# Three of the six chunks of each expert tile's down product as three fp32r products of high and low halves, the weights' low halves made by GpSimd

## What is computed

```python
def _expert(h, g, u, d):
    return jnp.einsum('...i,hi->...h', jax.nn.silu(h @ g.T) * (h @ u.T), d)
probs = jax.nn.softmax(x @ wr.T + rb, axis=-1)
scores, idx = jax.lax.top_k(probs, 2)
scores = scores / scores.sum(axis=-1, keepdims=True)
w = jnp.sum(scores[..., None] * jax.nn.one_hot(idx, 7, dtype=x.dtype), axis=-2)
for e in range(7):
    out = out + w[..., e:e + 1] * _expert(x, rg[e], ru[e], rd[e])
```

## Time and profile before

| | us |
|---|---|
| median of 3 runs | 1199.94 (1197.11 to 1203.04) |
| the profiled execution | 1197.35 |
| its span in the profile | 1195.5 |
| TensorE busy | 1064.4 (89%) |
| VectorE / ScalarE / GpSimd busy | 629.3 / 617.3 / 392.1 |
| routed stage, from the first tile's down product to the last but one | 42 of them, from 495.9 to 819.1 |

### The profile page before, as it was taken

The page is one execution under the profiler, slowest core; times in us unless marked ns, Lnnn a source line. Parts: engine busy times, 40 slices in busy tenths (PEclk is TensorE's granted clock), DMA queues, the critical chain, the costliest instruction groups (busy, mean ns, idle before and its releaser), DMA issues.

```text
span 1195.5 us, 28362 instructions
## 1 busy us (share of the span) xinstructions
PE 1064.4 (89%) x10404; PEld 901.1 (75%) x10405; DVE 629.3 (53%) x1174; ACT 617.3 (52%) x1043; POOL 392.1 (33%) x271
## 2 busy tenths in 40 slices
PE   6988799888988887899999999995678899789998
PEld 5877677766766665788888888884467777689998
DVE  3337577643332324566666666662257766734443
ACT  3446566643533432455555555553255557556554
POOL 1155344424534443022221122222455455611110
PEclk9999899998998988899999999998789989889999
DMA  6550000053101112101110101102311000000000
GB/s 230 199 225 3 4 2 3 3 221 109 29 20 23 26 21 70 46 31 35 35 35 31 35 31 35 35 31 67 111 27 39 22 0 2 2 1 21 20 10 32
DMA packets 31010, 57.45 MB, mean 48 GB/s; under 512 B 13084, under 2 KB 22506, under 8 KB 29780
## 3 DMA queue, kind: packets, MB, share of 16 engines
q1 hardware_dynamic: 16376, 44.06, 11.1%
q0 software_dynamic: 13328, 10.66, 3.3%
q10 hardware_dynamic: 1228, 1.60, 0.4%
HBM read 41.51 MB, written 14.67 MB: 47 GB/s over the span
## 4 chain that ended last, share of the span: by engine, by line
PE 58%; DVE 11%; issue 9%; POOL 9%; ACT 9%; DMA 3%; SPq 0%; DVEq 0%; ACTq 0%; POOLq 0%
PE ps L1197 20%; PE ps L1202 11%; PE ps L1204 10%; PE ps L1203 10%; POOL routed_in L462 7%; DVE Sb L854 6%; PE ps L1576 2%; DVE mx L849 2%; ACT RTs L624 2%; PE ps L1308 1%; DMA x_in<-in_xT_dram 1%; ACT vts L604 1%; ACT RTs L622 1%; PE ps L1319 1%; ACT prs L610 1%
## 5 line engine op out<-in xcount | busy, mean ns | idle before, releaser
L486 POOL DMA_INDIRECT routed_out<-yt,tile_to x43 | 65.4, 1521 | 289.5 <-DVE yt L1132 285.3
L1110 DVE TENSOR_TENSOR tile_w<-arena,tile_w 128x1408 fp32r<-128x1408 f32 x86 | 139.3, 1621 | 35.6 <-ACT tile_w L784 35.6
L1197 PE MATMUL ps<-arena,shared 128*128 x516 | 130.9, 395 | 1.0 <-ACT shared L780 1.0
L1202 PE MATMUL ps<-tile_w,xTs 128*128 128x352 f32 x344 | 120.1, 349 | 2.4 <-DVE xTs L1115 2.4
L784 ACT ACTIVATE tile_w<-arena 128x1408 fp32r x86 | 118.2, 1375 | 6.5 <-issue 6.5
L949 DVE TENSOR_TENSOR Hd<-Sg,ps 128x296 f32<-128x296 f32 x96 | 44.3, 462 | 140.1 <-ACT Sg L725 135.4
L773 ACT ACTIVATE shared<-ps 128x352 f32<-128x352 f32 x86 | 39.8, 463 | 145.8 <-PE ps L1204 141.4
L1204 PE MATMUL ps<-tile_w,xTs 128*128 128x352 f32 x344 | 112.0, 326 | 0.0
L1197 PEld LDWEIGHTS ps<-arena,shared 128*128 128x128 f32 x516 | 90.9, 189 | 28.0 <-issue 15.6
L1203 PE MATMUL ps<-tile_w,xTs 128*128 128x352 f32 x344 | 111.9, 325 | 0.0
L389 POOL TENSOR_TENSOR xn<-cen,rsd 128x592 f32<-128x592 f32 x32 | 46.7, 1460 | 191.1 <-ACT rsd L572 191.0
(11 more groups left out here) (195 smaller groups left out, 2673.1 us busy)
## 6 DMA issues: line engine op xcount, KB each, us to landing
arena<-in_ew_dram SPq DMA_DIRECT2D x7, 2176.0 KB, 13.4
x_in<-in_xT_dram SPq DMA_DIRECT2D x7, 888.0 KB, 5.7
xt<-routed_in SPq DMA_DIRECT2D x43, 129.0 KB, 2.0
yg<-routed_out SPq DMA_DIRECT2D x8, 512.0 KB
out_dram<-h SPq DMA_DIRECT2D x8, 296.0 KB, 2.7
routed_in<-zero_x SPq DMA_DIRECT2D x13, 129.0 KB, 10.3
gu_i<-in_gu_dram SPq DMA_DIRECT2D x1, 1536.0 KB, 10.2
shared<-in_gu_dram SPq DMA_DIRECT2D x1, 1408.0 KB, 7.4
```

Source lines behind the costliest of these rows:

```text
L486: pool.indirect_dma_start(ys, bass.IndirectOffsetOnAxis(tile_to[b][:, 0:1], 0), yt[b][:], None).then_inc(s_yt, 16)
L1110: dve.tensor_tensor(tile_w[half][1], gate_up_of(w, half), tile_w[half][0].bitcast(F32), ALU.subtract).then_inc(s.wl, 1)
L1197: return pe.matmul(out_, lhsT, rhs, start=start, stop=stop)
L1202: pe.matmul(out_, w[1], x[0], start=start, stop=False)
```

## The change

Chunks 0 to 2 of the down product become `mm3` products; chunks 3 to 5 stay `mm`, and are now first. For that

- ScalarE makes `dn_hi`, the high half of the down weights' first three chunks (128 x 768), once per tile at the head of its step, after the down product that used it before (`E.y_mm`). It copies the transposes in three pieces instead of two: `HT_hi` (128 x 384, fp32r), then two pieces of `HTs`.
- VectorE makes `HT_lo` (128 x 384, from PSUM and `HT_hi`) between `lower_weights` and `gate(t, 1)`.
- GpSimd makes `dn_lo` in two instructions (128 x 512 and 128 x 256, reading `arena` and `dn_hi`) at the head of `store(t)`, ahead of the wait for `yt`; it also loads the register with the tile's weight offset.
- TensorE waits for `E.htl` and `E.dl` between the three `mm` and the nine fp32r matmuls.

The core of the diff:

```diff
+SPLIT = 3
...
+                def lower_down(t):
+                    w = weights_of(pool, t)
+                    pool.wait_ge(E.dh, t + 1)
+                    dn_w = down_of(w)
+                    pool.tensor_tensor(dn_lo01, dn_w[:, 0:2], dn_hi[:, 0:2].bitcast(F32), ALU.subtract)
+                    pool.tensor_tensor(dn_lo[2], dn_w[:, 2], dn_hi[:, 2].bitcast(F32), ALU.subtract).then_inc(E.dl, 1)
+
                 def store(t, b):
+                    lower_down(t)
                     pool.wait_ge(E.y, FREE + t + 1)
                     pool.sem_inc(s_turn, 1)
...
                 def hidden_t(t):
 
                     act.wait_ge(s.ht_mm, t + 1)
-                    act.activation(HTs[:, 0:5], ps[:, 4:6, :].rearrange("p b (j m) -> p (b j) m", m=P)[:, 0:5],
-                                   ACT.Copy)
-                    act.activation(HTs[0:I0 - 5 * P, 5], ps[0:I0 - 5 * P, 5, P:2 * P], ACT.Copy).then_inc(s.ht, 1)
+                    in_bank = lambda bk, n: ps[:, bk, 0:n * P].rearrange("p (j m) -> p j m", m=P)
+                    act.activation(HT_hi, in_bank(4, SPLIT), ACT.Copy).then_inc(s.ht, 1)
+                    act.activation(HTs[:, 0:5 - SPLIT], in_bank(5, 5 - SPLIT), ACT.Copy)
+                    act.activation(HTs[0:I0 - 5 * P, 5 - SPLIT], ps[0:I0 - 5 * P, 5, 2 * P:3 * P], ACT.Copy).then_inc(s.ht, 1)
+
+                def upper_down(t):
+
+                    w = weights_of(act, t)
+                    act.wait_ge(s.y_mm, t)
+                    act.activation(dn_hi, down_of(w), ACT.Copy).then_inc(s.dh, 1)
...
                 def step(t, b, last):
+                    upper_down(t - 1)
...
+                def lower_hidden(t):
+                    dve.wait_ge(s.ht, FREE + 2 * t + 1)
+                    dve.tensor_tensor(HT_lo, ps[:, 4, 0:SPLIT * P].rearrange("p (j m) -> p j m", m=P), HT_hi.bitcast(F32),
+                                      ALU.subtract).then_inc(s.htl, 1)
...
                     gate(t, b, 0)
                     if not last:
                         lower_weights(t + 1, w, 0)
+                    lower_hidden(t - 1)
                     gate(t, b, 1)
...
                 def tile_out(t, w):
-                    pe.wait_ge(s.ht, FREE + t + 1)
+                    pe.wait_ge(s.ht, FREE + 2 * t + 2)
                     pe.wait_ge(s.y, FREE + t)
-                    for j, r in enumerate(hidden_chunks(I0)):
-                        ins = mm(ps[:, 7, 0:D], HTs[0:r, j], arena[0:r, bass.ds(w + DK * 2 * I0 + j * D, D)],
-                                 j == 0, j == 5)
+                    for j, r in list(enumerate(hidden_chunks(I0)))[SPLIT:]:
+                        mm(ps[:, 7, 0:D], HTs[0:r, j - SPLIT], arena[0:r, bass.ds(w + DK * 2 * I0 + j * D, D)],
+                           j == SPLIT, False)
+                    pe.wait_ge(s.htl, FREE + t + 1)
+                    pe.wait_ge(s.dl, t + 1)
+                    for j in range(SPLIT):
+                        ins = mm3(ps[:, 7, 0:D], (HT_hi[:, j], HT_lo[:, j]), (dn_hi[:, j], dn_lo[j]), False, j == SPLIT - 1)
                     ins.then_inc(s.y_mm, 1)
```

More of the change, by code:

```diff
@@ L176, in vit_kernel @@
         Hdt = [shared[:, (1 + b) * I0:(2 + b) * I0] for b in range(2)]
-        HTs = shared[:, 3 * I0:3 * I0 + 6 * P].rearrange("p (j m) -> p j m", j=6)
-        assert 3 * I0 + 6 * P + 4 * D <= EW
+        HTs = shared[:, 3 * I0 + SPLIT * P:3 * I0 + 6 * P].rearrange("p (j m) -> p j m", m=P)
+        HT_hi = nc.alloc_sbuf_tensor_at("HT_hi", [P, SPLIT, P], F32R, offset=shared_at + 4 * 3 * I0)[:]
+        HT_lo = nc.alloc_sbuf_tensor_at("HT_lo", [P, SPLIT, P], F32R, offset=norm_at + 4 * 8 * DK * IH)[:]
+        assert prs_at - norm_at - 4 * 8 * DK * IH >= 4 * SPLIT * P
+        tail_at = shared_at + 4 * (3 * I0 + 6 * P)
+        assert 3 * I0 + 6 * P + D + 4 * D <= EW
         xt = [sb(f"xt{b}", [P, XW]) for b in range(2)]
         yt = [sb(f"yt{b}", [P, D]) for b in range(2)]
+        sg_at = -(-nc.sbuf_base // 32) * 32
         Sg = [sb(f"Sg{b}", [P, N]) for b in range(2)]
         Hd = [sb(f"Hd{b}", [P, N]) for b in range(LAG + 1)]
+        hidden_free = nc.sbuf_base
+        assert hidden_free - sg_at >= 5 * 4 * D and shared_at + 4 * EW - tail_at >= 4 * D
+        dn_hi = nc.alloc_sbuf_tensor_at("dn_hi", [P, SPLIT, D], F32R, offset=sg_at)[:]
+        dn_lo01 = nc.alloc_sbuf_tensor_at("dn_lo01", [P, 2, D], F32R, offset=sg_at + 4 * SPLIT * D)[:]
+        dn_lo2 = nc.alloc_sbuf_tensor_at("dn_lo2", [P, D], F32R, offset=tail_at)[:]
+        dn_lo = [dn_lo01[:, 0], dn_lo01[:, 1], dn_lo2]
         r_w = sb("r_w", [P, DK, EXPERTS])
@@ L228, in vit_kernel @@
         F = [counted(ffn_sems + routing_sems, "f0_"), counted(ffn_sems, "f1_")]
-        E = counted("xt_mm gu_mm ht_mm y_mm wh wl xh xt sg hd ht y stored", "e_")
+        E = counted("xt_mm gu_mm ht_mm y_mm wh wl dh dl xh xt sg hd ht htl y stored", "e_")
         C = counted("mm0 mm1 sum h", "c_")
@@ L241, in gate_up_of, with down_of @@
             return arena[:, bass.ds(w, 2 * DK * I0)].rearrange("p (q i) -> p q i", i=I0)[:, :, half * IH:(half + 1) * IH]
+        def down_of(w):
+            return arena[:, bass.ds(w + DK * 2 * I0, SPLIT * D)].rearrange("p (j d) -> p j d", d=D)
         def norms_idle(eng):
@@ L489, in store @@
                     pool.sem_inc(E.stored, 1)
+                norms_idle(pool)
                 with pool.Fori(0, TILES // 2) as i:
@@ L813, in routed @@
                 over_tiles(act, step)
+                upper_down(TILES - 1)
                 hidden_t(TILES - 1)
@@ L1104, in routed @@
                 s = E
-                for buf_free in (s.xt, s.hd, s.y):
+                for buf_free in (s.xt, s.hd, s.y, s.htl):
                     dve.sem_inc(buf_free, FREE)
+                def lower_hidden(t):
+                    dve.wait_ge(s.ht, FREE + 2 * t + 1)
+                    dve.tensor_tensor(HT_lo, ps[:, 4, 0:SPLIT * P].rearrange("p (j m) -> p j m", m=P), HT_hi.bitcast(F32),
+                                      ALU.subtract).then_inc(s.htl, 1)
                 def lower_weights(t, w, half):
@@ L1158, in routed @@
                 over_tiles(dve, step)
+                lower_hidden(TILES - 1)
                 tile_out(TILES - 1, 0)
@@ L1573, in hidden_t @@
                     pe.wait_ge(s.hd, FREE + 2 * t + 2)
-                    pe.wait_ge(s.ht, FREE + t)
+                    pe.wait_ge(s.ht, FREE + 2 * t)
+                    pe.wait_ge(s.htl, FREE + t)
                     for j, r in enumerate(hidden_chunks(I0)):
-                        ins = pe.transpose(ps[0:r, 4 + j // 4, (j % 4) * P:(j % 4 + 1) * P],
+                        ins = pe.transpose(ps[0:r, 4 + j // SPLIT, (j % SPLIT) * P:(j % SPLIT + 1) * P],
                                            Hdt[b][:, j * P:j * P + r], ident)
```

## The result

| | before | changed |
|---|---|---|
| median, us | 1201.49 (4 runs) | 1256.89 (4 runs, 1253.08 to 1258.6) |
| ratio, 95% interval | | 1.0462 (1.0433 to 1.0492) |
| span of the profiled execution | 1195.5 | 1256.2 |
| mean distance of two stores' starts, tiles 0 to 40 | 7.82 | 9.10 |

The change costs 4.6%. The direction was forecast, the size was not: 36 us were forecast, 55 came, and 1256.89 lies above the range (1209 to 1252). Between the two profiled executions lie 60.7 us. Of these, 52.3 lie between the first store and the last but one, where 32.8 were forecast, 4.5 at the end of the stage, 2.3 ahead of the first store and 1.6 behind the last one.

What follows compares the result with a forecast made beforehand. TensorE bounds the kernel before; after the change a ring through GpSimd's store and subtractions does. 41 steps x 0.80 = 32.8 us, plus 3.7 at the end, less 0.4 for the first tile, is 36.1 us: 1236 us, range 1209 to 1252.

Steps and rivals of the forecast that it cites:

- a ring: Routed stage: store, landing, GpSimd's subtractions, nine matmuls, `yt`, next store follow one another, none hidden; 8.62 us a step.
- The ring's length: Time from one store's start to the next in the routed stage: 8.62 instead of 7.81 us, 0.80 more.
- the second of the sum: GpSimd's first subtraction waits for VectorE's L1110, which frees the way at S + 3.9; register load hidden, up to 0.65 us.
- the sign that the register load was too low: Check in the changed kernel's profile: GpSimd's L503 starting later than 0.9 us after the store's landing.
- a rival for a longer ring: Longer register load, VectorE not moving forward or slower subtractions: 0.25 to 0.55 us a step, 1246 to 1258 us; chance 0.12.
- the clock rival: TensorE's idling over 1 us drops its clock to 0.50 in every step: 155 us more, 1355 us; chance 0.05.
- the 1.6 I named: Check: GpSimd's L503 lasts some 1.6 us or more instead of 1.26, beginning before VectorE's L1110 ends.
- the 0.65 of the sum: Wait of GpSimd's subtraction for VectorE's first-half instruction, up to 0.65 us a step, with the register load hidden under it.
- The first rival: GpSimd's subtraction is not held up by VectorE's L1110: 0.15 to 0.45 us a step more, 1209 to 1222 us; chance 0.14.
- TensorE's saving: Down product: three `mm` go, 1.45 us, nine fp32r matmuls come, 1.08 us; TensorE's work falls 0.37 us a tile.
- the faster rival: TensorE stays the bound and its saving of 0.37 us a tile counts: 15.6 us less, 1184 us; chance 0.04.
- The end of the stage: Last result of the routed stage goes around without VectorE's part: 3.1 to 4.3 us more, 3.7 taken.

Runs made afterwards that it cites:

- e1_floor: Changed kernel with GpSimd making the low half of the down weights once, before its loop (stale results); 1193.64 us, 0.9942 of the kernel before.
- e5_before_store: Changed kernel with GpSimd making the next tile's low half ahead of the store; 1195.55 us, 0.9964 of the kernel before.
- e11_load: Changed kernel, three chunks, with TensorE's load of the weight offset moved behind the step's transposes; 1250.28 us, 1.042 of the kernel before.
- e3_no_vector_lock: Changed kernel with VectorE's first-half weight subtraction in the loop on 8 columns instead of 1408; 1247.01 us, 1.0392 of the kernel before.
- e2_no_register: Changed kernel with GpSimd's subtraction at constant offset 0, so it loads no register; 1250.43 us, 1.0415 of the kernel before.
- e6_two_chunks: Changed kernel with two chunks of the six as fp32r products instead of three (SPLIT = 2); 1223.12 us, 1.0168 of the kernel before.
- e4_before_landing: Changed kernel with GpSimd making the next tile's low half after issuing the store, before waiting for its landing; 1209.91 us, 1.0084 of the kernel before.
- e7_no_register_no_vector: Changed kernel with GpSimd at constant offset 0 and VectorE's first-half subtraction on 8 columns; 1217.59 us, 1.0137 of the kernel before.
- e10_two_chunks_load: Changed kernel with two fp32r chunks and TensorE's weight-offset load moved behind the step's transposes; 1204.96 us, 1.0047 of the kernel before.

## Why the prediction was wrong in size

**What bounds, and that a ring forms: right.** TensorE's L1243 was released by L504 before all 42 down products and idled about 1 us; the landing, GpSimd's register load and the subtractions lie in the chain in the order given. VectorE's instruction is not in it, since no semaphore ties it to GpSimd; it shows in the length of L503. e1_floor and e5_before_store show it as the cause.

**The ring's length: 8.62 forecast, 9.10 measured, 0.48 x 41 = 19.5 us, nearly all that the medians lack (55 less 36).** By its steps, for the two turns of the loop:

| from the store's start S | forecast | turn 1 | turn 2 |
|---|---|---|---|
| landing | 3.0 | 2.97 | 2.98 |
| GpSimd ready (start of L503) | 3.25 to 4.1 | 3.94 | 4.18 |
| VectorE's first-half instruction lets go (0.15 before its end) | 3.9 | 4.03 | 4.43 |
| second subtraction ends | 5.85 | 5.99 | 6.39 |
| first fp32r matmul | 5.90 | 6.14 | 6.54 |
| next store | 8.62 | 8.79 | 9.19 |

The step that failed is the second of the sum: VectorE's first-half instruction moves forward with TensorE's step and lets go at S + 3.9, and the register load hides under it up to there. Both halves of it were wrong.

- VectorE's instruction moved forward by 0.13 us in one turn, and back by 0.27 in the other, where TensorE's step starts 0.4 us late, so it let go at S + 4.03 and S + 4.43. It was the later of the two in both turns. The cause I had not seen at all: TensorE's own register load and branch at the head of its step, as I read it hidden behind fp32 passes before and bare after the wait. e11_load takes that gap away. There L1149 lets go at S + 3.95 in both turns, nearly as forecast, and the regular turns are 8.71 and 8.92 us, 0.18 less on average.
- The register load takes 0.73 us, with the loop's branch 0.96, and GpSimd is ready at S + 3.94 and S + 4.18, where 3.9 was the limit. The changed kernel hides this, but it is the floor when VectorE is not in the way: the regular turns of e3_no_vector_lock and e11_load stay at 8.80 and 8.81 us on average, 0.18 over the forecast.

The prediction named a start of L503 later than 0.9 us after the landing as the sign that the register load was too low; it came, with 0.97 and 1.20 us. The wake after GpSimd's signal was 0.15 us instead of 0.05, and from the first fp32r matmul to the next store it took 2.65 us instead of 2.72. I had a rival for a longer ring, 1246 to 1258, by a longer register load or a VectorE that does not move forward, and gave it 0.12. It is what happened, and the result is inside it; its chance was too low.

**Irregular steps.** The mean of the two turns is 8.99; the last 0.1 us a step, some 4 us, comes from single steps. Three take over 10 us and give most of it, 3.6 us. In three others, of 9.45 to 9.66 us, the store took longer to land, as the chain shows for one of them (2.97 us is usual):

```profile
693.32 3.68 DMA routed_out<-yt,tile_to
```

Why these stores land late is open. Two windows of one of the three longest steps show the clock (granted clock is the third number from the end):

```profile
529.00:530.00 1.00, 1.00 (x5) 1.00 (x5) 0.72 (x1) 0.00 (x0) 0.98 (x1) 0.50 0.00 0
531.00:532.00 1.00, 1.00 (x9) 0.93 (x8) 0.00 (x0) 0.40 (x2) 0.00 (x0) 0.76 0.32 131
```

So the clock rival was right in kind in three steps of 42, not in each as it was priced. TensorE's matmuls at half the clock then delay VectorE past GpSimd's first subtraction, and VectorE gets in ahead of the second:

```profile
533.22 1.28 POOL L503 TENSOR_TENSOR dn_lo<-arena,dn_hi 128x512 fp32r<-128x512 f32 x1 [2.63 <-issue]
534.46 2.10 POOL L504 TENSOR_TENSOR dn_lo<-arena,dn_hi 128x256 fp32r<-128x256 f32 x1
...
533.47 2.51 DVE L1149 TENSOR_TENSOR tile_w<-arena,tile_w 128x1408 fp32r<-128x1408 f32 x1 [0.73 <-ACT tile_w L816]
```

**GpSimd's subtraction and VectorE's instruction.** The one waits for the other: right, as the earlier trace rows had it. L503 mostly lasted 1.34 to 1.37 us in one turn and 1.48 to 1.54 in the other, less than the 1.6 I named, because it came late. Nearly taking VectorE's instruction away gave 0.19 us a step alone, not the 0.65 of the sum, because GpSimd, held by its own register load, was ready only 0.1 to 0.25 us earlier than VectorE let go. The first rival (GpSimd comes through beside VectorE) is refuted by e2_no_register, where L503 starts early and takes 2.08 us.

**TensorE's saving: 0.37 forecast, 0.13 measured.** I divided 2.90 us by twelve passes and took 0.242 for each. Six passes fewer took 1.29 us away, 0.215 each, and the first distance behind the fp32 ones is longer than the others (0.22 us instead of 0.12 in e1_floor), which makes 1.16 for nine instead of 1.08. This had no weight in the forecast, since it was hidden, but it made the faster rival, 1184, too good: the best versions reach 1193.6. Per fp32r matmul 0.120 us was right (0.12 measured).

**The end of the stage: 3.7 forecast, 4.5 measured.** The difference is the clock again. Before the last down product TensorE waits 3.75 us for GpSimd, and behind that its granted clock is 0.50 (1.2 GHz). The fp32r matmuls start 0.21 us apart instead of 0.12, which adds some 0.9 us for nine:

```profile
881.08 0.55 PE L1243 MATMUL ps<-dn_hi,HT_lo 128*128 128x256 f32 x1 [3.75 <-POOL dn_lo L504]
881.42 0.41 PE L1244 MATMUL ps<-dn_lo,HT_hi 128*128 128x256 f32 x1
881.64 0.41 PE L1245 MATMUL ps<-dn_hi,HT_hi 128*128 128x256 f32 x1
```

ScalarE and VectorE: their added instructions cost nothing that can be seen, as forecast. The start of the first store, 2.3 us later in the changed kernel's trace, is not explained; in the other runs it lies anywhere between 498.7 and 505.1, so it need not come from the change. The 0.4 us that the first tile was to save would be lost in that.

## What to carry to other kernels

A subtraction on an idle engine is free only where it stands in that engine's order: behind a wait for a DMA's landing it made a ring that no engine's busy time shows. Add up such a ring from the start of one turn to the next, with the register load and the loop's branch of every engine in it, and then look where else in the order the new work can stand; here moving a few lines turned 4.6% lost into 0.5% won. Two waits that end together hide each other: taking away either showed 0.13 to 0.19 us a step, both 0.95. Compare the regular turns too, and not only their mean: there the register load alone was worth 0.02 us.

## What the runs showed of the hardware

- The load of one register from SBUF costs GpSimd 0.73 us between a landing and its next instruction (0.97 to 0.24 with a constant offset). On TensorE it shows behind a wait, at the head of a step: with the loop's branch as a gap of 0.50 us (changed kernel) or 0.73 us (e6_two_chunks) where 0.12 is usual, without the branch not at all in the changed kernel and as 0.39 us in e6_two_chunks. Moved behind the transposes it shows nowhere.
- Two GpSimd instructions in a row can let a waiting instruction of VectorE in between. It got in where it was waiting (L504 2.10 and 2.13 us instead of 0.72), and in other steps of e4_before_landing the second subtraction went first by 0.02 us and VectorE's instruction took 2.20 instead of 1.62 us.
- An indirect DMA on GpSimd takes 2.33 us to issue in e5_before_store, 1.57 in the changed kernel, and 0.98 at 884.68, where VectorE does nothing. The difference is about what VectorE's instruction on two tensors of SBUF still had to run: 1.47 us (602.70 to 604.17) and 0.71 us (611.49 to 612.20).
- TensorE's granted clock fell to 0.50 in three places of the changed kernel's routed stage, with pauses of about 1 us in every step before them, and once more behind the pause of 3.75 us at its end. In e1_floor, without pauses, it stayed at 1.00 from 500 to 800 us, and so it did in e4_before_landing, e6_two_chunks, e7_no_register_no_vector and e10_two_chunks_load, where the pauses are shorter. No run changes the pauses alone, so this is an observation.
